# First quad's maxima from float32 products, two powers, later expert weights, last inverses spread by TensorE, in a new order of work

## What is computed

```python
xn = layernorm(x)
x = x + attention_0(xn) + block(xn)       # causal attention, 16 heads of 8 channels
                                          # block: a second causal attention with biases, then
                                          # 8 experts (128 -> 512 -> 128, exact gelu), the top 2 by a router
xn = layernorm(x)
x = x + attention_1(xn) + experts_1(xn)   # attention without a mask; 8 experts, tanh gelu, top 2
# each attention, for each head:
logits = q @ k.T / sqrt(8); attn = softmax(logits); out = attn @ v
```

## Time and profile before

| | us |
|---|---|
| median of 3 runs | 717.04 (716.78 to 718.7) |
| the profiled execution, its own time | 717.42 |
| its span, first to last instruction | 715.7 |
| TensorE busy (matmuls) | 688.1 |
| VectorE busy | 564.3 |
| ScalarE busy | 522.7 |
| GpSimd busy | 192.7 |

### The profile page before, as it was taken

The page is one execution under the profiler, slowest core; times in us unless marked ns, Lnnn a source line. Parts: engine busy times, 40 slices in busy tenths (PEclk is TensorE's granted clock), DMA queues, the critical chain, the costliest instruction groups (busy, mean ns, idle before and its releaser), DMA issues.

```text
span 715.7 us, 27610 instructions
## 1 busy us (share of the span) xinstructions
PE 688.1 (96%) x12078; PEld 346.0 (48%) x12078; DVE 564.3 (79%) x1089; ACT 522.7 (73%) x645; POOL 192.7 (27%) x457
## 2 busy tenths in 40 slices
PE   6589999999999999999999999999999999999996
PEld 2243444575644545446444355366554646533234
DVE  6689998365799987778999787687886676899966
ACT  6278877855677757777787968767889767688892
POOL 5255545212341211212444000212453001110000
PEclk9569999999999999999999999999999999999999
DMA  5453514010130211030133100220122000030011
GB/s 137 120 145 96 162 41 115 19 64 21 29 93 2 56 43 46 18 101 24 35 105 93 40 19 7 70 57 18 30 75 77 3 4 19 23 90 15 13 41 41
DMA packets 42150, 39.52 MB, mean 55 GB/s; under 512 B 14360, under 2 KB 37328, under 8 KB 41808
## 3 DMA queue, kind: packets, MB, share of 16 engines
q1 hardware_dynamic: 40688, 36.20, 17.9%
q10 hardware_dynamic: 1152, 1.05, 0.6%
q0 software_dynamic: 192, 0.52, 0.2%
HBM read 10.47 MB, written 1.44 MB: 17 GB/s over the span
## 4 chain that ended last, share of the span: by engine, by line
PE 83%; DVE 9%; ACT 3%; issue 2%; DMA 1%; POOL 1%; ACTq 0%; SPq 0%; DVEq 0%; POOLq 0%
PE psum L865 45%; PE psum L964 16%; PE psum L943 9%; PE psum L916 9%; DVE neg_max L558 4%; ACT probs L811 2%; PE psum L921 2%; DVE acc L713 2%; PE psum L881 1%; DMA q_stack<-part 1%; DMA heads_raw<-head_sums 0%; DVE normed_y L468 0%; POOL rstd L1076 0%; DVE normed_x L468 0%; DVE stats L445 0%
## 5 line engine op out<-in xcount | busy, mean ns | idle before, releaser
L558 DVE TENSOR_REDUCE neg_max<-psum 128x2 f32<-128x1024 f32 (+2 forms) x320 | 345.4, 1112 | 76.3 <-PE psum L921 46.9
L811 ACT ACTIVATE probs<-psum 128x1024 f32<-128x1024 f32 (+1 forms) x320 | 288.1, 938 | 96.6 <-PE psum L943 95.1
L964 PE MATMUL psum<-probs,v_ones 128*32 128x512 f32 (+3 forms) x1536 | 158.4, 496 | 0.1
L835 ACT ACTIVATE probs<-psum,col 128x512 f32<-128x512 f32 x160 | 100.2, 685 | 55.5 <-PE psum L865 55.2
L1115 POOL TENSOR_SCALAR_AFFINE_SELECT probs<-probs 128x512 f32<-128x512 f32 x128 | 81.4, 640 | 189.2 <-ACT probs L811 186.7
L865 PE MATMUL psum<-ew,probs 128*32 128x128 f32 x4096 | 124.9, 274 | 0.0
L916 PE MATMUL psum<-k_stack,q_stack 64*128 64x512 bf16 (+3 forms) x768 | 115.3, 336 | 8.0 <-DMA q_stack<-part 4.4
L865 PEld LDWEIGHTS psum<-ew,probs 128*32 128x32 f32 x4096 | 109.5, 110 | 18.1 <-issue 15.3
L865 PE MATMUL psum<-normed_T_a,ew 128*32 128x512 f32 x1024 | 117.7, 593 | 0.0
L943 PE MATMUL psum<-q_stack,k_stack 64*128 64x512 bf16 (+3 forms) x768 | 110.8, 330 | 4.0 <-DVE neg_max L558 2.2
L753 ACT ACT_TABLE_LOAD x70 | 89.8, 1283 | 1.2
(11 more groups left out here) (134 smaller groups left out, 474.0 us busy)
## 6 DMA issues: line engine op xcount, KB each, us to landing
q_stack<-part SPq DMA_DIRECT2D x66, 128.0 KB, 2.5
k_stack<-part SPq DMA_DIRECT2D x66, 128.0 KB, 2.5
heads_raw<-head_sums SPq DMA_DIRECT2D x24, 128.0 KB
heads_inv<-inverses SPq DMA_DIRECT2D x12, 256.0 KB, 3.3
ew<-w_expert_in SPq DMA_DIRECT2D x4, 512.0 KB, 4.6
ew<-w_expert_out SPq DMA_DIRECT2D x4, 512.0 KB, 5.3
q_stack<-k_stack SPq DMA_DIRECT2D x14, 128.0 KB, 2.5
q_stack<-maxT SPq DMA_DIRECT2D x48, 32.0 KB, 1.9
```

The lines of the kernel that those rows point to most:

```text
L558: eng.tensor_reduce(neg_max[:, q % 2, :, xs[0]:xs[-1] + 1, i], src, AX_X, ALU.max, negate=True).then_inc(vector_done.sem, 1)
L811: eng.activation(dst, src, ACT.Exp, scale=SCALE).then_inc(probs_ready.sem, 1)
L835: ins = eng.activation(probs[:, order.slot[step[:-1]], 2 * k + f, :], two_banks(step)[:, f, :], ACT.Gelu_apprx_tanh if layer else ACT.Gelu ...
L964: ins = eng.matmul(sum_bank[32 * c:32 * c + V_COLS, q0:TILES * P], v_ones[u][:, j, g // 2 * QH + c, col0:col0 + V_COLS], probs[:, order.sl ...
```

## The change

Six edits. (1) For the first quad of the first attention only, queries and keys are projected once more (`first` 0 and 1) with weights sorted so that each of the four heads has 32 partitions, 8 of them used (`proj_first`). VectorE copies the queries twice, once with the odd heads' rows set to zero and once with the even ones' (`head_of_row`), ScalarE copies the keys, and `max` of this quad multiplies these float32 tiles, 64 partitions at a time, in place of the bf16 stack. The stack is first waited for by the `max` of quad 1 or by `scores` (`stack_landed`). (2) The power is taken in two halves of 128x4; normed x waits for the first alone. (3) The pieces of expert weights are issued later: the first at step 78 of the list, behind the third `max_turn`, the last at step 309. (4) For the last attention, `heads_spread` replaces the way of the inverses through memory: 32 float32 matmuls of 64 columns spread them by a 0/1 matrix (`spread`, made by GpSimd) into a bank, from which VectorE multiplies. (5) `heads_inverse` waits for the sums alone (`sums_landed`), `heads_norm` for the rest. (6) The sorting of the weights of u = 1 and 2 and the clearing of the second key stack are steps of their own (chain C), and the whole list `SCORE` has a new order, of which the first and the last of 13 lines stand here.

```diff
@@ chains
-        front += [("turn", b, "x"), ("project", b, 0, 0), ("project", b, 0, 1), ("second", b, 0, 0),
+        front += [("turn", b, "x")] + ([("first", b, 0), ("first", b, 1)] if b == 0 else []) + [("project", b, 0, 0), ("project", b, 0, 1), ("second", b, 0, 0),
...
+        spread = [("heads_write", b, u), ("heads_read", b, u), ("heads_norm", b, u)]
+        heads += [("heads_sort", b, u, 0), ("heads_sort", b, u, 1), ("heads_inverse", b, u),
+                  *(spread if (b, u) != ATTENTIONS[-1] else [("heads_spread", b, u)]), ("out_project", b, u)]
...
+        "A": front, "C": [("sort", 0, 1), ("clear_keys", 1), ("sort", 0, 2)], "F": ffn, "G": gates, "H": heads,
@@ SCORE
-AAAAAAAA6A6A0AKAAAKA1KA6A6M2M4M0M2M4M0A6M2AALM4AT6M0M2AM4KM0M2S4A6S0M4LS2M0S4AM2T6M0S4AM2VAM4KM0S2M4S2VM0S2M4KVS0M2T
+AAAAAAAA6A6CA0CA1A6M2AAKAAKM4A0A6M2M4M0A6M2KCA4AAM0KM2T6AM4M0M2M4AA6S0S2M4M0AS4M2KS0AT6M4S2M0M4S2VM0M2AS4VM0AT6S4M2V
...
-S0VT6HS4S2VH6S0S4GVS2S0G6VS4GS2GJ6VS0S4HS2VVJ4VJ6G5HI0HI2G6HJ0J6HJ1J0HJ6H1G
+2VS4M2S0H6S4GG2GVT6GS0S2S4J6VVS0S2S4VJ6S0S2VG6S4S0VG6S2VJ6VHHI4HI0J6H4J5J6J4H5J6G
@@ vector
+            for head in range(P // HEAD_ROWS):
+                for x in range(2):
+                    eng.memset(head_of_row[HEAD_ROWS * head:HEAD_ROWS * (head + 1), x:x + 1], float(head % 2 == x))
+            eng.memset(proj_first[:, :, :], 0.0)
...
+                elif kind == "first" and step[2] == 0:
+                    src = bank(step)
+                    eng.wait_ge(vector_done.sem, 1)
+                    for x in range(2):
+                        eng.tensor_scalar(q_first[x][:, :], src, head_of_row[:, x:x + 1], None, ALU.mult)\
+                           .then_inc(vector_done.sem, 1)
+                        n = vector_done.count()
+                    order.work_freed[step] = order.dve[step] = n
...
-                        eng.wait_ge(heads_landed[pair].sem, 32 * (n_heads + 1))
+                        eng.wait_ge(sums_landed[pair].sem, 16 * (n_heads + 1))
...
+                    inv = heads_inv[:, :] if kind == "heads_norm" else bank(step)
+                    eng.tensor_tensor(headsT[:, :], heads_raw[:, :], inv, ALU.mult).then_inc(vector_done.sem, 1)
@@ scalar
-                    clear_keys(0)
+                    clear_keys(b)
...
+                    for k in range(2):
+                        eng.activation(
+                            proj_first[:, k, :].rearrange("p (a x d) -> p a x d", a=2, x=2)[:, :, :, 0:HD],
+                            raw_qk[:, 0, k, 0:HALF].rearrange("p (d x a o) -> p o a x d", d=HD, x=2, a=2)[:, 0],
+                            ACT.Copy).then_inc(first_sorted.sem, 1)
...
-                    clear_keys(1)
+                elif kind == "sort":
+                    eng.wait_ge(loaded, 16 * N_LOADS)
+                    sort_heads(step[2])
+                elif kind == "first" and step[2] == 1:
+                    eng.wait_ge(work_full.sem, order.work[step] + 1)
+                    eng.activation(k_first[:, :], one_bank(step), ACT.Copy).then_inc(scalar_done.sem, 1)
...
-                elif kind == "turn" and (b, step[2]) == (0, "h"):
-                    eng.wait_ge(loaded, 16 * N_LOADS)
-                    sort_heads(1)
-                    sort_heads(2)
@@ tensor
+            stacks_read = set()
+            def stack_landed(b, u):
+                slot = order.stacks[b, u]
+                if (b, u) not in stacks_read:
+                    stacks_read.add((b, u))
+                    eng.wait_ge(sync_landed[slot].sem, 16 * order.q_landed[b, u])
+                    eng.wait_ge(keys_landed[slot].sem, 16 * order.k_landed[b, u])
+                    if (b, u) in FIRST_FILLS:
+                        eng.wait_ge(blocks_landed[slot].sem, 32)
+                        eng.wait_ge(thirds_landed[slot].sem, 32)
...
+                elif kind == "first":
+                    k = step[2]
+                    eng.wait_ge(first_sorted.sem, 2)
+                    eng.wait_ge(vector_done.sem, order.dve["turn", b, "x"])
+                    ins = columns(bank(step), proj_first[:, k, :], normed_T["x"][:, :])
...
+                    if q > 0:
+                        stack_landed(b, u)
+                    elif (i, k) == (0, 0):
+                        eng.wait_ge(made.sem, N_MADE)
+                        eng.wait_ge(vector_done.sem, order.dve["first", b, 0])
+                        eng.wait_ge(scalar_done.sem, order.act["first", b, 1])
...
-                            ins = eng.matmul(dst[:, a, col0:col0 + keys],
-                                             q_stack[slot][rows_of, head, i * P:(i + 1) * P],
-                                             k_stack[slot][rows_of, head, 0:keys], start=True, stop=not CAUSAL[u])
+                            queries = q_stack[slot][rows_of, head, :] if q else q_first[x][rows_of, :]
+                            seen = k_stack[slot][rows_of, head, 0:keys] if q else k_first[rows_of, 0:keys]
+                            ins = eng.matmul(dst[:, a, col0:col0 + keys], queries[:, i * P:(i + 1) * P], seen,
+                                             start=True, stop=not CAUSAL[u])
...
+                elif kind == "heads_spread":
+                    eng.wait_ge(vector_done.sem, order.dve["heads_inverse", *step[1:]])
+                    eng.wait_ge(spread_made.sem, 1)
+                    dst = bank(step)
+                    for n in range(HD):
+                        for c in range(COLUMN_TILES):
+                            some = slice(COLUMN * c, COLUMN * c + COLUMN)
+                            ins = eng.matmul(dst[some, HALF * n:HALF * n + HALF], spread[:, n, some], heads_den[:, :],
+                                             start=True, stop=True)
@@ gpsimd
-                    eng.tensor_tensor(rstd_of[n_set][:, :, :], var_eps_of[n_set][:, :, :], minus_half[:, 0:2 - n_set, :], ALU.pow)\
-                       .then_inc(gpsimd_done.sem, 1)
-                    assert gpsimd_done.count() == order.pool[step]
+                    for n in range(2 - n_set):
+                        eng.tensor_tensor(rstd_of[n_set][:, n, :], var_eps_of[n_set][:, n, :], minus_half[:, 0, :], ALU.pow)\
+                           .then_inc(gpsimd_done.sem, 1)
...
+                    eng.tensor_copy(spread[:, :, :].rearrange("p n (m d) -> p n m d", d=HD),
+                                    ident[:, :].rearrange("p (m n) -> p n m", n=HD).unsqueeze(3)
+                                    .to_broadcast([P, HD, HEADS, HD])).then_inc(spread_made.sem, 1)
```

More of the change, by code:

```diff
@@ L237, in __init__ @@
                 self.q_landed[b, u], self.k_landed[b, u] = q_count[slot], k_count[slot]
[L238 removed]
+            if kind in ("second", "gate_exp") or kind == "first" and step[2] == 1 or kind == "project" and step[3] < 2 and step[1:3] in CAST_BY_SCALAR or kind == "values" and step[3] % 2 == 1 and step[4] == TILES - 1 or \
                     kind == "clear_v" and step[2] > 0:
@@ L262, in build @@
         bias_qk = sb("bias_qk", [P, 2])
+        head_of_row = sb("head_of_row", [P, 2])
         ew1 = sb("ew1", [P, EXPERTS, 4, P])
@@ L465, in _ @@
                         eng.wait_ge(gpsimd_done.sem, order.pool["bias", b - 1, 1])
-                    eng.wait_ge(gpsimd_done.sem, order.pool["norm", b, "x" if what == "h" else what])
+                    eng.wait_ge(gpsimd_done.sem, order.pool["norm", b, what])
                     for t in range(TILES):
```

109 lines of the change are left out of this document (66 added, 43 removed).

## The result

The changed kernel took 715.64 us (median of 22 executions, 712.73 to 718.34) against 718.27 for the kernel before beside it (22 executions): a ratio of 0.9967, 95% interval 0.9956 to 0.9979. A second comparison gave 716.25 against 717.45, ratio 0.9983 (0.9969 to 0.9997). So it is faster by 1.2 to 2.6 us, where 5.7 were forecast. The profiled execution took 716.6 us, with a span of 714.9.

The account below looks back on a forecast made before the run. TensorE, busy 688.1 of 715.7 us, was taken as the bound, with time to win at head and tail. 717.42 - 5.3 (head) - 0.4 (tail) = 711.7, and 0.4 lower for the median: 711.3 us, range 707.5 to 716.5.

Parts of the forecast that it names:

- The middle, reordered: Between head and tail: same work in another order, taken as 0, from -4 to +2 us gained.
- Rival D: Middle: the new order makes TensorE wait where VectorE is nearly full; 9.8 us added, time 721; chance 0.12.
- First quad without its stack: Head: float32 maxima without waiting for the stack bring quad 1 to 26.9 us from 32.2, lead 5.3 us.
- No wait to speak of: Head: the first stack's last transfers land at 26 to 26.5 us, so quad 1 hardly waits for them.
- common point: Point of equal work in both orders, here VectorE's first max of quad 1, at 32.18 us before.
- rival C: Head: the stack lands at 29 us, quad 1 waits 2.4, lead 2.9, time 713.7; chance 0.10.
- rival A: Head: TensorE's clock stays up from 12 us on; head gains 7.3, time 709.3; chance 0.17.
- Rival B: Head: the clock falls at 17 us all the same; lead 1.4, time 715.2; chance 0.10.
- Two powers: Start: halved power gains 0.64 us, nine memsets cost part; net 0.2 gained, bounds -0.4 and +0.5.
- Expert weights later: Loads issued after the head: nothing waits for them; nothing gained beyond the stack's earlier landing, nothing lost.
- b: Head: the first stack's transfers, without weights ahead, take 2.5 to 3 us and land at 26 to 26.5.
- Last inverses: Tail: the memory round trip was hidden, only order wins; 0.4 us gained, bounds -1.0 and +0.8.

Follow-up runs that it names:

- The mirror: Kernel before with one move, GpSimd's parts (1, 0) directly behind norm (0, a): 719.96 us, ratio 1.0031 to the kernel before.
- e8: Changed kernel with parts (1, 0) moved before turn (0, a) and parts (3, 1) before max (1, 2, 0, 0, 1): 712.23 us, ratio 0.9926.
- e2: Changed kernel with the first quad's maxima taken from the bf16 stack again, float32 tiles still made: 725.1 us, ratio 1.0105.
- e1: Changed kernel with parts (1, 0) moved before turn (0, a) and parts (3, 1) before values (2, 0, 2, 1): 711.80 us, ratio 0.9921.
- e1b: The same kernel as e1, run again beside other kernels: 713.85 us, ratio 0.9941.
- e5: Changed kernel with one power of 128x8 in place of two of 128x4: 717.89 us, ratio 1.0010.
- e4: Changed kernel with the first load of expert weights back ahead of the last issue of the first stack: 719.13 us, ratio 1.0018.
- e3: Changed kernel with the last attention's inverses sent through memory and the multiplication behind three expert outputs, as before: 717.99 us, ratio 1.0009.
- e6: Changed kernel with parts (1, 0) as in e1 and parts (3, 1) further back, before values (2, 0, 3, 0): 717.44 us, ratio 0.9993.
- e9: Changed kernel with only parts (3, 1) moved, to its place in e8, and parts (1, 0) left as it was: 714.71 us, ratio 0.9954.

## Why the prediction was wrong

Forecast were 711.3 us and a gain of 5.7; the time was 715.64 and the gain 1.2 to 2.6, less than half. The range held the time, and the direction was right. In the two profiles, 0.8 us apart, the head gained 4.7 for 5.3 and everything behind it lost 3.9 where 0.4 were to be gained.

- **The middle, reordered ("Same work, other order ... Taken as 0")** is the step that failed. Up to the last copy of maxima it lost 5.7 us, 3.1 between the ninth and the twelfth copy and 2.6 behind the twelfth; a tail 1.8 us shorter hid part of it. The mechanism is no lack of slack on TensorE, which the step looked at, but two engines that hold each other up: VectorE's operations from SBUF to SBUF beside GpSimd's subtractions. The mirror put it into the kernel before (+2.2 us), and taking both meetings out of the changed kernel gave 712.23 us, 0.9 over the forecast, with a middle 0.5 us shorter than the old one (e8). So 0 was right for the order without its two meetings. In the profiles the bound of this step, a loss of 4, was passed, and only the better tail kept the total within it. The trace of before had only weak signs: its longest `normed_a`, `normed_x`, `normed_y` and `normed_h` took 0.65 to 0.81 us where the median was 0.34 to 0.35. But the two lists could be compared, and the new one puts two `parts` right behind a `norm` of another batch.
- **Rival D** had the right place to look, the middle, and the wrong mechanism and size: no uniform loss, but one meeting of 2.2 us with up to 1.6 more for the clock, one of about 1, and a stack whose price is open.
- **First quad without its stack** was right in its mechanism: first `max` matmul at 13.71 (about 14 was forecast), stack there at 26.2 (26 to 26.5), first reduction of quad 1 at 26.63 (26.9), ninth copy at 89.92 (about 89), lead 4.7 (5.3). e2 shows that the float32 products carry it. Their price held too: two heads of 512 columns kept TensorE for 0.94 us (19.48 to 20.42), 0.9 was taken. But part of the agreement is luck. "No wait to speak of" was wrong: project 0 was out at 12.88 and not 13.8, VectorE had done its work by 25.44, and then it stood still for 1.18 us and TensorE for 2.43, until the stack was there. So the stack set the common point, and not VectorE's sum of 26.9; rival C had such a wait, though for a stack at 29 us. And the stack came in time by two errors that cancel: its last issue began at 22.23, about 0.5 us earlier than taken, and landed after 3.7 us in place of 2.5 to 3.
- **The clock** of the head was between forecast and rival A: 1.00 from 12 to 28 us, then 0.50 to 0.54 to about 40, with 0.69 from 24.6 to 46.4. Rival B did not occur. The Trainium skill ("TensorE: Matmul & The Clock Gate", What's actually happening) would have had A as the forecast: the trace agrees from 12 to 28 us and not from 28 to 40. But the bounds of the lead were the right thing to give: e1 and e1b are one kernel, and their ninth copies lie 3.2 us apart, with no other difference than the clock in their windows.
- **Two powers**: 0.2 gained was forecast. In the profile the turned x is copied at 9.20 for 9.15 before; VectorE's statistics ended 0.7 us later (6.06 for 5.37), for which 0.45 had been taken, and the nine memsets took what the power gave. The result stays within the bounds. One power in the changed kernel costs 1.9 to 3.1 us in the median and 0.9 at the ninth copy (e5), so the split may be worth more than its 0.64 us; the interval leaves that open.
- **Expert weights later**: no wait of their own, as said; what they do for the landing of the stack (b, and rival C, priced at 2.4) was right in kind. e4 puts them back and loses 2.5 to 3.7 us.
- **Last inverses ("replacing it wins nothing by itself")** was wrong in its mechanism. The round trip itself ended early, but to be hidden behind three expert outputs is to stand behind them: the multiplication and the projection came forward in VectorE's queue only with the short way. e3 measures 1.7 us. The chain behind the last values was forecast at 12.7 and took 11.7. The stretch behind the last copy of maxima is 1.8 us shorter (27.42 for 29.23, where 0.4 were forecast), but ten more steps of the list lie ahead of it, so a part of that is work moved forward. That the reciprocal waits for the sums alone (edit 5) was not tried by itself.
- **TensorE's idle time from 64 to 690** was to be near 5 us and was 9.3 (626.0 less 616.74), against 5.1 before. That number alone told the loss; it is 4.96 in e8.

## What to carry to other kernels

When an order is rewritten, look in both lists for the pairs of steps that hold each other up and not only for dependencies: two subtractions of GpSimd put right behind the power that releases VectorE's SBUF-to-SBUF work more than doubled that work's time here (1.42 to 3.17 us), and slowed nothing beside work from PSUM. Each such step has a window, not only a latest time: too early it collides, too late a buffer that it reads (`rest`) holds up its next writer, and here the place that collides and the one that comes too late lay 12.2 us apart (369.1 in e1 and 381.3 in e6), 2.5 of which are the earlier start of e1's whole stretch (normed a at 368.58 for 371.08). And a round trip that no one waits for may still keep a multiplication late in a queue.

## What the runs showed of the hardware

VectorE and GpSimd held each other up. Four multiplications of 128x128 from SBUF to SBUF went from 1.42 to 3.17 us, and the longest single one took 1.2 us where the median is 0.34, while GpSimd's two subtractions were not slowed: they took 2.27 us there and 2.28 beside work from PSUM. It went both ways with another pair. An addition with two inputs in SBUF went from 0.68 to 1.13 beside causal cuts of GpSimd, which were themselves stretched from 0.64 to 0.83 each (two in 1.67 us at 114.57). The Trainium skill ("SBUF — State Buffer", SBUF: two separate sides) has the pair of ports that the two engines share as an exclusive lock, held for the whole instruction, and names VectorE's operations with two SBUF inputs among those that need it. The traces agree with the lock, since a multiplication that meets a subtraction of 1.14 us takes up to 1.2; the multiplication has one SBUF tensor and two columns of scalars as inputs, and whether it counts by its inputs or by its mode no run here shows.

The granted clock was not the same in all executions of one kernel. Between 8 and 16 us it was 1.00 in e1 and 0.57 in e1b, one and the same kernel; behind the collision it fell to 0.59 in the changed kernel and stayed at 1.00 in e9 with the same wait of 2.27 us of TensorE. What decides between the two was not found.
